# Attention's drain: which out-projection products run where, and when the transposed outputs are fetched

## The reference, cut to what matters

```python
scores = jnp.einsum('bqhd,bkhd->bhqk', q_full, k_full) * softmax_scale
scores = jnp.where(causal[None, None], scores, jnp.finfo(scores.dtype).min)
attn = jax.nn.softmax(scores, axis=-1)
out = jnp.einsum('bhqk,bkhd->bqhd', attn, v).reshape(B, S, H * VD)
return out @ wo.T
```

## Time and profile before

| | |
|---|---|
| median of 3 runs | 1631.84 us (1630.63 to 1632.85) |
| the profiled execution | 1631.13 us, its span 1629.3 us |
| mean granted TensorE clock | 0.992 of full speed |
| busy over the span | PE 95%, DVE 63%, ACT 53%, POOL 50% |
| attention's units | 4.5 us each with a query projection |
| last score matmul to the first matmul of out_projection | about 1060 to 1089.6 us |

### The profile page before, as it was taken

The page is one execution under the profiler, slowest core; times in us unless marked ns, Lnnn a source line. Parts: engine busy times, 40 slices in busy tenths (PEclk is TensorE's granted clock), DMA queues, the critical chain, the costliest instruction groups (busy, mean ns, idle before and its releaser), DMA issues. The chain is left out here.

```text
span 1629.3 us, 31927 instructions
## 1 busy us (share of the span) xinstructions
PE 1547.9 (95%) x12366; PEld 950.2 (58%) x12366; DVE 1018.8 (63%) x2747; ACT 868.9 (53%) x1654; POOL 811.3 (50%) x699
## 2 busy tenths in 40 slices
PE   5898899999989999999999999889999999999998
PEld 4655455555556776777777777644444444465554
DVE  7898857776778888888888888832110010344433
ACT  6886222221759999999999999931210000211110
POOL 4223244444957888888888888830010000244440
PEclk9999899999999999999999999999999999999999
DMA  9894334444756999999998999997763331233331
GB/s 359 297 330 149 91 88 107 143 142 128 154 120 112 187 173 189 179 184 187 195 190 174 184 185 173 178 208 226 176 167 80 101 91 26 75 66 84 83 86 65
DMA packets 560263, 249.82 MB, mean 153 GB/s; under 512 B 502256, under 2 KB 535152, under 8 KB 559984
## 3 DMA queue, kind: packets, MB, share of 16 engines
q1 hardware_dynamic: 560112, 247.78, 66.1%
HBM read 73.68 MB, written 48.23 MB: 75 GB/s over the span
## 5 line engine op out<-in xcount | busy, mean ns | idle before, releaser
L1967 POOL TENSOR_TENSOR xb<-xb 128x1280 f16<-128x1280 f32 x128 | 335.6, 2622 | 7.8 <-ACT xb L1870 7.8
L1862 ACT ACTIVATE xb<-bk,D_sv,qw_c 128x512 f32<-128x512 f32 (+3 forms) x512 | 289.3, 623 | 4.4 <-DVE D_sv L1925 4.2
L1916 DVE TENSOR_REDUCE bk<-bk 128x1 f32<-128x512 f32 (+3 forms) x512 | 228.3, 492 | 20.5 <-PE bk L1812 19.9
L92 POOL TENSOR_SCALAR mv<-mv 128x1 f32<-128x1 f32 x64 | 31.2, 488 | 279.1 <-DVE mv L87 278.1
L1870 ACT ACTIVATE xb<-xb 128x1280 f16<-128x1280 f32 x128 | 162.7, 1271 | 13.1 <-DMA xb<-xb 9.3
L1803 PE MATMUL bk<-kTh,D_QTh 128*128 128x512 f16 (+3 forms) x512 | 153.4, 300 | 6.3 <-ACT xb L1862 6.2
L1804 PE MATMUL bk<-kTl,D_QTh 128*128 128x512 f16 (+3 forms) x512 | 153.2, 299 | 0.0
L1805 PE MATMUL bk<-kTh,D_QTl 128*128 128x512 f16 (+3 forms) x512 | 146.5, 299 | 0.0
L1827 PE MATMUL D_t<-vh,xb 128*128 128x65 f16 x1280 | 131.5, 194 | 4.7 <-DMA xb<-xb 3.0
L1828 PE MATMUL D_t<-vl,xb 128*128 128x65 f16 x1280 | 131.6, 193 | 0.0
L1829 PE MATMUL D_t<-vh,xb 128*128 128x65 f16 x1280 | 131.0, 193 | 0.0
(11 more groups left out here) (331 smaller groups left out, 4383.9 us busy)
## 6 DMA issues: line engine op xcount, KB each, us to landing
od<-D_os SPq DMA_DIRECT2D x32, 512.0 KB, 4.5
xd<-xb SPq DMA_DIRECT2D x16, 512.0 KB, 4.2
ow_raw<-mwd SPq DMA_DIRECT2D x16, 512.0 KB, 4.7
xb<-xd SPq DMA_DIRECT2D x16, 512.0 KB, 5.9
out_x<-xb SPq DMA_DIRECT2D x16, 512.0 KB, 3.0
xb<-in_x SPq DMA_DIRECT2D x6, 1024.0 KB, 13.6
A_wo<-in_wo SPq DMA_DIRECT2D x6, 1024.0 KB, 7.5
ow_raw<-in_w SPq DMA_DIRECT2D x16, 384.0 KB, 4.3
```

The costliest lines, as they stand in the source:

```text
L1862: m = e.activation(p[:, AT[i]:AT[i] + N], Sb[n % 4][:, c:c + N], ACT.Exp, scale=qw.col(qw.NEG, g), bias=s[:, 7 - i:8 - i])
L1916: m = e.tensor_reduce(minima(u, i), Sb[n % 4][:, c:c + N], AX.X, ALU.min)
L1967: e.tensor_tensor(P2[u % 3][:, 1280:2560], P[u % 3][:, :], P2[u % 3][:, 0:1280], ALU.subtract).then_inc(s_pl, 1)
```

## The change

Three things in two blocks:

1. Tile 2's first four steps leave the drain. Product (2, kt) for kt = 0 to 3 now stands inside `scores(u)` for u = 124 to 127, between part 0 and part 1. Its banks qb0, qb1 are free once the last query projection is consumed.
2. The steps of tiles 0 and 1 start one iteration sooner: u = 128 to 131 in place of 129 to 132, two products an iteration in place of three. The wait for the last exponentials (`s_exp`, `s_bias`) now stands at u = 128. Iteration 132 holds only `values(127)`.
3. Quarters 0, 1 and 2 of the three tiles are fetched during attention: u = 42, 48, 54, then 74, 80, 86, then 106, 112, 118, each behind a wait for stores made many units before. Only quarter 3 is left to `out_projection`.

```diff
@@ scores(u) of attention, pe
                     e.matmul(ps, ql, kT[0][:, k0:k0 + M], start=False, stop=False)
                     c += M
+                if part == 0 and u >= NU - ow.AHEAD:
+
+                    w.wait_ge(s_qn, NU)
+                    w.wait_ge(s_qm, NU)
+                    ow.pe_product(e, w, 2, u - NU + ow.AHEAD)
             w.wait_ge(s_hide, 2)
@@ the loop over u of attention, pe
-            if NU < u <= NU + ow.AHEAD:
+            if NU <= u < NU + ow.AHEAD:
                 w.wait_ge(s_exp, 3 * NU)
                 w.wait_ge(s_bias, 2 * NU)
-                w.wait_ge(s_qn, NU)
-                w.wait_ge(s_qm, NU)
-                for j in range(ow.G):
-                    ow.pe_product(e, w, j, u - NU - 1)
+                for j in range(2):
+                    ow.pe_product(e, w, j, u - NU)
@@ the loop over u of attention, sp
-            if u == NU - 5:
-
-                w.wait_ge(s_ot[0], 16 * 15)
-            if NU - 5 <= u < NU - 5 + ow.G:
-                ow.sp_turn_piece(e, u - NU + 5, 0)
-            if NU + 2 <= u < NU + 2 + ow.G:
-                ow.sp_turn_piece(e, u - NU - 2, 1)
+            for p in range(3):
+                for j in range(ow.G):
+                    if u == 42 + 32 * p + 6 * j:
+
+                        w.wait_ge(s_ot[0], 16 * (4 * p + 3))
+                        ow.sp_turn_piece(e, j, p)
@@ out_projection, sp
-        for p in range(2, 4):
-            if p == 3:
-                w.wait_ge(ow.s_o[0], 16 * G)
-            for j in range(G):
-                ow.sp_turn_piece(e, j, p)
-                ow.sp_load(e, w, next(loads))
+        w.wait_ge(ow.s_o[0], 16 * G)
+        for j in range(G):
+            ow.sp_turn_piece(e, j, 3)
+            ow.sp_load(e, w, next(loads))
```

## The result

| | before | after |
|---|---|---|
| median of 22 executions each, in turn | 1632.05 us (1630.22 to 1633.52) | 1628.66 us (1626.83 to 1631.34) |
| ratio of the means, 95% interval | | 0.9982 (0.9976 to 0.9989), 2.9 us less (1.8 to 3.9) |
| the profiled execution, its span | 1631.13, 1629.3 us | 1629.54, 1627.7 us |
| mean granted TensorE clock of it | 0.992 | 0.991 |

The forecast was 1629.7 us, in a range of 1626.3 to 1633.8. The medians lie 3.4 us apart, the means (1631.91 and 1629.06 us) 2.9.

What follows compares the result with a forecast made beforehand. PE, busy 95% of the span, was taken to bound the kernel. Drain and block's end (-6.1 us), clock (+2.4) and quarters (+1.6) sum to -2.1, from 1631.84 to 1629.7 us; range 1626.3 to 1633.8 us.

Steps and rivals of the forecast that it cites:

- Tile 2 in units 124 to 127: Last four attention units: products partly fill PE's idle time, cost the softmax 0.4 us net, take 5.2 us from the drain.
- Tiles 0 and 1 sooner: Drain: PE works 14.1 us without a gap after the last exponentials; `values(127)` ends 5.8 us sooner, at 1079.3.
- The gain up to out_projection: From drain to PE's first matmul of `out_projection`: it starts near 1083.5 instead of 1089.59, 6.1 us sooner.
- The block's end: Behind `values(127)`: 3.8 us to SP's last issue plus 0.45 us of barrier, PE idle about 4.2 us.
- The clock: Start of `out_projection`: the idle 4.2 us brings the lower clock level, costing +2.4 us, bounds 0 and 3.4.
- the clock holds: Rival at the block's end: no clock loss, or a late one; 1625.7 to 1627.3 us; chance 0.22.
- The clock falls twice: Rival at the hand-over to the drain: waits there also bring the lower level, +2.5 us, 1632.2 us; chance 0.10.
- The nine quarters: Attention loop: fetches delay turns, mostly at u = 42, costing PE +1.6 us in all, bounds 0 and 4.
- quarters cost more than their cover: Rival in the attention loop: each quarter costs PE 1.1 us, nine cost 9.9, total 1638.0 us; chance 0.10.
- out_projection's queue: SP's queue in `out_projection`: three quarters less ahead of its weight loads, worth nothing since PE idles nowhere there.
- The change does what it says: Units 124 to 127: exponentials end by 1065.1; the rival has them later, 1631.9 us, chance 0.06.
- The sum: Whole kernel: -6.1 + 2.4 + 1.6 = -2.1 us, from 1631.84 to 1629.7 us.

Runs made afterwards that it cites:

- fetches alone: Against before: only the change's quarter fetches inside attention, all products where they stood before; 1630.19 us, ratio to before 1.000.
- tile 2 alone: Against the change: steps of tiles 0 and 1 back at u = 129 to 132, tile 2's products and the fetches kept; 1627.69 us, ratio to before 0.9976.
- filler at the exit: Against the change: 17 matmuls of 512 columns, whose result nobody reads, added behind `values(127)`; 1627.19 us, ratio to before 0.9981.
- quarter 0 alone in the loop: Against the change: only quarter 0 fetched in the loop, quarter 1 at u = 130 to 132, quarter 2 in `out_projection`; 1627.62 us, ratio to before 0.9984.
- fetches apart: Against the change: quarters moved to u = 44, 48, 52, 76, 80, 84, 108, 112, 116, away from loads and stores; 1627.71 us, ratio to before 0.9981.
- last step behind: Against the change: the last of the four steps of tiles 0 and 1 moved behind `values(127)`; 1623.75 us, ratio to before 0.9961, 5 executions.
- loads sooner: Against last step behind: the two weight loads that end the block issued at u = 131, ahead of the last store; 1623.73 us, ratio to before 0.9964.
- together: Against loads sooner: quarters also moved away from iterations with loads and stores, as in fetches apart; 1622.82 us, ratio to before 0.9953.

## Why the prediction was right, point by point

**Tile 2 in units 124 to 127: right, and cheaper than forecast.** The forecast was that exponentials end 0.4 us later net. They end 0.1 us sooner relative to the loop (29.4 against 29.5 us), and the 5.2 us of products are out of the drain. The fetches alone show two parts of about 0.8 us that cancel, the products' cost and the late turns'. The room was read from one unit: the 4.13 us of the earlier trace rows hold for units 124 and 125, while from unit 121 to unit 124 the starts were 3.25 to 4.34 us apart.

**Tiles 0 and 1 sooner: the number right, the reason not quite.** Forecast: 14.1 us without a gap from the last exponentials to the end of `values(127)`. Measured: 14.22 in every trace with all four steps ahead of `values(127)`. But the mechanism I gave, PE with work enough, is only half of it. Without the earlier start (tile 2 alone) it takes the same 14.22 us, with PE waiting for DVE's release of the output bank, and DVE for POOL. The two limits lie on top of each other; a kernel that took more work off PE ahead of `values(125)` would have gained nothing, where my sum would have promised a gain.

**The gain up to out_projection: 5.6 us by means, not 6.1.** The step compared with one trace of before, whose drain of 20.40 us was the longest of three (20.40, 19.91, 18.51). The 3.03 us wait of the earlier trace rows was 2.32 us in the third:

```profile
1067.77 0.24 PE L1827 MATMUL D_t<-vh,xb 128*128 128x65 f16 x1 [2.32 <-DMA xb<-xb]
```

**The block's end: right.** Forecast 4.2 us of idle, measured 4.22.

**The clock: right in place, and in size in the traces.** Forecast +2.4 with bounds 0 and 3.4. The five traces with a bare exit lost 1.68, 2.85, 2.76, 2.57 and 1.41 us on the 36 matmuls, 2.25 in the mean; the covered exits lost none. The rival "the clock holds" falls. "The clock falls twice" didn't come in the change, and the fetches alone show that it was near.

The page "TensorE: Matmul & The Clock Gate" of the Trainium skill, Part 1, which the prediction set beside that rival, says that the throttled state is the default. The prediction's own reading of it, that any thin stretch is suspect, agrees with the two waits of 1.64 and 1.51 us in the fetches alone. It was too broad: after a single wait of 1.64 us in the change the clock stayed full.

**The nine quarters: right in the mean, with one condition misjudged.** Forecast +1.6 with bounds 0 and 4, nearly all of it at u = 42; measured +1.67 over seven traces, +0.24 when they stand apart. That the size fits is in part luck: the wait behind u = 42 grew from 1.5 to only 2.16 and 1.98 us, not to 3, while u = 74, where before had no wait, reached 2.72 and 1.59. The step's own price of 1.51 us was low where load and store stand beside it: 2.12 us at u = 42. On the Trainium skill's page "DMA: Bandwidth & Descriptors" (latency and other measured facts), 261 GB/s gave an estimate of 1.0 us for it; the rows stay above that, at 1.25 us of issue and more, so the row was the better price. The rival "quarters cost more than their cover" falls: nine cost 1.7 us, not 9.9.

**out_projection's queue: right.** From its 37th matmul on every trace takes the same time within 0.2 us.

**The change does what it says**: the idle time ahead of part 1 is gone and the exponentials are not late.

**The sum.** Forecast -2.1; traces -1.5, and the timed executions -2.9 (1.8 to 3.9). The last is within the stated range, though the traces' -1.5 lies below its interval. Pairs of kernels seem to say that two terms are nothing: fewer or quieter fetches (-1.1 and -1.4 in the traces) and the filler (-2.25) moved the ratio by 0.0002 at most. All kernels together say otherwise. In the table, *traces* is the sum of each kernel's stages against before, where the loop is the mean of all traces with the same fetches and the 36 matmuls behind a bare exit are the mean of five; *times* is the measured ratio with its interval, in us.

| kernel | traces | times |
|---|---|---|
| the change | -1.7 | -2.9 (-3.9 to -1.8) |
| quarter 0 alone in the loop | -2.8 | -2.6 (-4.1 to -1.1) |
| fetches alone | +0.9 | 0.0 (-1.6 to +1.5) |
| fetches apart | -3.1 | -3.1 (-4.6 to -1.6) |
| last step behind | -5.5 | -6.4 (-8.6 to -4.1) |
| tile 2 alone | -3.9 | -3.9 (-5.4 to -2.4) |
| filler at the exit | -3.9 | -3.1 (-4.6 to -1.6) |
| loads sooner | -6.7 | -5.9 (-8.2 to -3.7) |
| together | -8.1 | -7.7 (-9.8 to -5.4) |

All eight experiments lie within their intervals, and the change lies 0.1 us outside. Without the clock's term, quarter 0 alone (-5.1) and fetches apart (-5.4) would lie outside; without the loop's term, tile 2 alone and the filler (-5.6 each) would. So the times bear out both terms, as long as the drain and the exit count one to one. What stays open is the 1.2 us by which the change did better than its stages, on which both of those pairs lean.

## What to carry to other kernels

Where blocks end at a barrier, work taken from ahead of the last step only moves the idle time to the exit, and an exit of 4.2 us without work cost 1.4 to 2.9 us of clock behind it in the traces. So leave an independent product behind the last dependent one: that was worth another 3.4 us here (0.9982 to 0.9961; 0.9 to 5.9 us by the two intervals), as much as the whole change, for one moved step. By the traces 1.6 us of it is the chain and about 2.3 us the clock. Before crediting a gap to one resource, look at whether a second one (here POOL's low halves, ahead of DVE's release of a bank) would end at the same time.

## What was not expected of the hardware

- The lower clock level came behind 4.22 us of idle after full work, in the second wait of before (3.03, 3.11 and 2.32 us, each after a first wait and 1.1 us of work), and in the second of two waits of 1.64 and 1.51 us with 1.1 us of work between (fetches alone). In the first trace of before and in the fetches alone it was there before the wait had ended, at 0.50 and 0.53 in 1066 to 1067. It did not come in the change behind 1.64 us alone, nor in tile 2 alone behind 1.65, 1.11 and 1.38 us with 1.1 and 3.7 us of work between, nor behind 1.60 us after a step of 2.6 us (last step behind).
- The same idle time of 4.2 us cost 1.41 to 2.85 us in five executions of kernels that are alike there.
- The mean granted clock of an execution differs from one to the next of the same kernel: 0.990 to 0.995 in 26 executions of before, and its time with it. Over 138 executions of ten kernels, each taken against the mean of its own group, 0.001 more of clock went with 0.55 us less time. That is a third of the 1.6 us that the same share of the span would be. Where the rest goes is not shown. The lower level also stands at places before attention, and not at the same ones in each trace: in 483 to 488 the granted clock was 1.00 in the first trace of before and 0.66 in the third. So the mean clock of an execution does not measure the drain or the exit alone.
- A quarter's issue took 1.25 us at the start of `out_projection` (loads sooner), 1.51 us between two turns, 2.12 us right behind a load and a store.
